# A delta-rule loop over 64 tokens: the state read two steps back, outer products on GpSimd, the read-out on VectorE and GpSimd

## What is computed

```
u_t = v_t - f_t (S_{t-1} k_t)
S_t = f_t S_{t-1} + b_t u_t k_t^T
o_t = S_t q_t
```

## Time and profile before

| what | us |
|---|---|
| runs, lowest / median / highest | 1332.24 / 1338.23 / 1342.46 |
| profiled execution: span from its first to its last instruction | 1330.3 |
| busy in the span: TensorE / VectorE / ScalarE / GpSimd | 1176.4 / 797.4 / 585.9 / 510.6 |
| the loop's groups: line 1787 / 1790 / 1792 on VectorE, 128 of each | 87.4 / 93.1 / 87.8 |
| line 1457 / line 1466 on TensorE | 138.3 / 134.3 |
| line 1858 / line 1862 on GpSimd | 149.2 / 78.0 |
| fades, line 1692 on ScalarE | 104.0 |

### The profile page before, as it was taken

How to read it: one execution, slowest core, us unless ns; L and a number is a source line. 1 busy time by engine, 2 the same in 40 slices (tenths; PEclk the granted TensorE clock), 3 DMA queues, 4 the chain that set the end, 5 groups by cost and what they waited for, 6 DMA issues and landing times. The chain is left out here.

```text
span 1330.3 us, 25816 instructions
## 1 busy us (share of the span) xinstructions
PE 1176.4 (88%) x9667; PEld 923.4 (69%) x9667; DVE 797.4 (60%) x1835; ACT 585.9 (44%) x1480; POOL 510.6 (38%) x568
## 2 busy tenths in 40 slices
PE   6999997598999999989699999995899999879975
PEld 4666666598999999963355656664677777667653
DVE  4666665421212212177899999996577677533687
ACT  3445442111121121145677777772344434325455
POOL 0111111132333333254688888884212122101556
PEclk9999999699999999999799999997999999979985
DMA  4111100689888888379000000002000040017611
GB/s 143 45 48 33 49 13 13 257 334 373 327 328 318 323 328 325 118 199 286 36 0 1 1 0 1 1 1 81 11 13 10 10 191 9 2 34 300 204 49 64
DMA packets 82716, 162.30 MB, mean 122 GB/s; under 512 B 42977, under 2 KB 61537, under 8 KB 76577
## 3 DMA queue, kind: packets, MB, share of 16 engines
q1 hardware_dynamic: 63776, 114.44, 25.1%
q0 software_dynamic: 10224, 44.05, 8.6%
q10 hardware_dynamic: 8592, 2.16, 0.8%
HBM read 134.28 MB, written 26.35 MB: 121 GB/s over the span
## 5 line engine op out<-in xcount | busy, mean ns | idle before, releaser
L936 PE MATMUL banks<-rowsT,w_up 128*128 128x128 f32 x1716 | 199.7, 276 | 0.1
L936 PEld LDWEIGHTS banks<-rowsT,w_up 128*128 128x128 f32 x1716 | 196.5, 193 | 0.4 <-DMA w_up<-in_up_w 0.4
L1466 PEld LDWEIGHTS banks<-ys,ident 128*128 128x128 f32 x992 | 125.2, 191 | 95.6 <-POOL ys L1862 66.0
L1858 POOL TENSOR_TENSOR ys<-xT_d,q_by_time 128x1024 f32<-128x1024 f32 x63 | 149.2, 2368 | 36.6 <-ACT xT_d L1596 36.6
L1466 PE MATMUL banks<-ys,ident 128*128 128x64 f32 x992 | 134.3, 290 | 17.7 <-POOL ys L1862 17.6
L1457 PE MATMUL banks<-made,ident 128*128 128x512 f32 x256 | 138.3, 622 | 12.0 <-DVE made L1792 11.9
L1692 ACT ACTIVATE banks<-banks,rate 128x256 f32<-128x256 f32 x256 | 104.0, 444 | 65.4 <-DVE made L1787 65.4
L1105 DVE TENSOR_TENSOR hT<-banks,silu 64x128 f32<-64x128 f32 x39 | 11.0, 283 | 164.8 <-ACT silu L993 164.8
L950 PE MATMUL banks<-w_down,hT 128*128 128x256 f32 x468 | 107.5, 379 | 0.6 <-DVE res L1115 0.6
L1790 DVE TENSOR_REDUCE banks<-made 128x32 f32<-128x544 f32 x128 | 93.1, 728 | 4.4
L878 POOL DMA_DIRECT2D w_down<-in_down_w x39 | 22.4, 574 | 186.6 <-PE banks L950 178.5
(11 more groups left out here) (325 smaller groups left out, 2383.0 us busy)
## 6 DMA issues: line engine op xcount, KB each, us to landing
w_up<-in_up_w SPq DMA_DIRECT2D x39, 1408.0 KB, 5.9
w_down<-in_down_w POOLq DMA_DIRECT2D x39, 768.0 KB, 5.2
inter<-res_x SPq DMA_DIRECT2D x16, 512.0 KB, 3.5
back<-inter SPq DMA_DIRECT2D x15, 512.0 KB, 4.0
patches<-in_patches SPq DMA_DIRECT2D x16, 384.0 KB, 3.3
f<-in_f SPq DMA_DIRECT2D x6, 1024.0 KB, 11.0
ys<-token_rows SPq DMA_DIRECT2D x16, 256.0 KB, 2.9
xn_rows<-xn_all SPq DMA_DIRECT2D x16, 128.0 KB, 1.7
```

The costliest lines, as they stand in the source:

```text
L936: ins = pe.matmul(out[:, m * P:(m + 1) * P], w[:, c, m * P:(m + 1) * P], x[:, c, :], start=(c == 0), stop=(c == 1))
L1466: ins = pe.matmul(o_sum[t % 2], ident[:, :], products[t % 2][:, :, :, n], start=(n == 0), stop=(n == FOLDED - 1))
L1858: pool.tensor_tensor(qs[:, :, :, :], Sc[(t + 1) % 2][:, :, :, :], bcast(qt[:, t, :, :], 2, HD), ALU.mult).then_inc(sem("qs_made"), 1)
```

## The change

- The loop reads the state two steps back. With S_{t-1} = f_{t-1} S_{t-2} + b_{t-1} u_{t-1} k_{t-1}^T put into the first equation, u_t needs S_{t-2} times a key scaled by both decays, plus a "link" number (from f_t, b_{t-1} and the product of neighbouring keys) times u_{t-1}. `prod` gets an 18th column: 16 products, the link term, the value. `prod`, `u` and `outer` become rings of two; `u` moves from PSUM to SBUF.
- Ahead of the loop, GpSimd multiplies neighbouring keys (`multiply_neighbours`, 1008 elements a group), VectorE sums them and makes the link numbers (`link_keys`), two small operations more in `scale_keys`, whose factor for `kb` now comes first; the link numbers take the place of the write rates in `rate`.
- GpSimd makes the outer product of all four groups in one operation, after the link term; it reads out group 3 (256 elements, from a copy that ScalarE makes) two steps behind.
- VectorE reads out groups 0 to 2 from PSUM in one operation (768 elements), three steps behind; the fold is gone.
- TensorE sums sixteen products for two tokens at once (128 columns), eight matmuls a step; ScalarE stores two tokens at once.
- ScalarE's fade comes after the product that reads the same state; it turns the queries of all four groups. The last two tokens are read out whole by VectorE. The chunks of squares move from 17, 34, 51 to 18, 36, 52.

The diff, cut to what the text speaks of:

```diff
-CUTS = (0, 17, 34, 51)
+CUTS = (0, 18, 36, 52)
 IN_STEPS = len(CUTS) - 1
-LASTS = ((CUTS[-1], TOK - 2), (TOK - 2, TOK))
+TAIL = 2
+LASTS = ((CUTS[-1], TOK - TAIL), (TOK - TAIL, TOK))
 LAST = TOK - CUTS[-1]
-FOLDED = HD // 2
+ROW = HD + 2
+DIRECT = CG - 1
...
+    link = rate[:, :, 0, :]
-    o_sum = [banks[:, b, 0:CG * HD].rearrange("p (g v) -> p g v", g=CG) for b in (5, 7)]
-    u = banks[:, 4, 0:CG * HD].rearrange("p (g v) -> p g v", g=CG)
+    o_sum = [banks[:, b, 0:2 * CG * HD] for b in (5, 7)]
...
         def add_outer(t, h):
...
+            if t:
+                pe.wait_ge(sem(f"faded{h}"), t)
+            pe.wait_ge(sem("outer_made"), t + 1)
+            pe.matmul(S[t % 2][:, halves[h], :, :], ident[:, :], outer[t % 2][:, halves[h], :, :], start=False,
                       stop=True, skip_group_check=True).then_inc(sem(f"state{h}"), 1)
...
+        def sum_pair(n, half):
+            if half == 0:
+                pe.wait_ge(sem("q_made"), 2 * n + 2)
+                pe.wait_ge(sem("q_copy_made"), 2 * n + 2)
+                if n > 1:
+                    pe.wait_ge(sem("o_made"), n - 1)
+            for k in range(HD // 2 * half, HD // 2 * (half + 1)):
+                ins = pe.matmul(o_sum[n % 2].rearrange("p (s n) -> p s n", s=2), ident[:, :],
+                                products[:, n % 2, :, :, k], start=(k == 0), stop=(k == HD - 1))
+            if half:
+                ins.then_inc(sem("o_summed_pair"), 1)
...
             for h in range(2):
                 add_outer(t, h)
-                if t >= 2:
-                    sum_folded(t - 2, h)
+            if t >= 3:
+                sum_pair((t - 3) // 2, (t - 3) % 2)
...
+        def place_values(t):
+            act.copy(prod[t % 2][:, :, :, HD + 1], v[:, :, :, t]).then_inc(sem("values_placed"), 1)
+        def fade(t, h):
+            act.wait_ge(sem(f"state{h}"), t + 1)
+            act.wait_ge(sem(f"prod_made{h}"), min(t + 2, TOK))
+            if t >= 2:
+                act.wait_ge(sem("q_made"), t - 1)
+            for g in (2 * h, 2 * h + 1):
+                ins = act.activation(S[t % 2][:, g, :, :].rearrange("p v k -> p (v k)"),
+                                     S[(t + 1) % 2][:, g, :, :].rearrange("p v k -> p (v k)"), ACT.Copy,
+                                     scale=rate[:, g, 1, t:t + 1])
+            ins.then_inc(sem(f"faded{h}"), 1)
+        def copy_last_group(j):
+            act.wait_ge(sem("state1"), j + 2)
+            if j >= 2:
+                act.wait_ge(sem("q_copy_made"), j - 1)
+            act.copy(Sc[j % 2], S[j % 2][:, DIRECT, :, :]).then_inc(sem("state_copied"), 1)
+        def store_pair(n):
+            act.wait_ge(sem("o_summed_pair"), n + 1)
+            act.copy(o[:, :, :, 2 * n:2 * n + 2], o_sum[n % 2].rearrange("p (s g d) -> p g d s", s=2, g=CG)
+                     ).then_inc(sem("o_made"), 1)
...
+        place_values(0)
+        place_values(1)
+        turn_queries(3)
         for t in range(TOK):
...
+            if t + 2 < TOK:
+                act.wait_ge(sem("u_made"), t + 1)
+                place_values(t + 2)
+            if t:
+                fade(t, 0)
+                fade(t, 1)
+            if 0 < t < TOK - 1:
+                copy_last_group(t - 1)
+            if t >= 5 and t % 2:
+                store_pair((t - 5) // 2)
...
         def scale_keys(g):
             dve.wait_ge(sem(f"rates{g}"), 16)
+            if g >= 2:
+                dve.wait_ge(sem("kb_made"), g - 1)
+            by_rate, by_rn = f[:, 0, g % 2, :], f[:, 1, g % 2, :]
+            dve.scalar_tensor_tensor(out=by_rn, in0=rate[:, g, 0, :], scalar=1.0, in1=rn[:, g, :],
+                                     op0=ALU.add, op1=ALU.mult).then_inc(sem("kb_scale"), 1)
             once.mark(dve.tensor_scalar(rate[:, g, 1, :], rate[:, g, 1, :], 0.5, 0.5, ALU.mult, ALU.add))
             once.settle()
-            once.mark(dve.scalar_tensor_tensor(out=f[:, 0, g % 2, :], in0=rn[:, g, :], scalar=-1.0, in1=rate[:, g, 1, :],
+            once.mark(dve.scalar_tensor_tensor(out=by_rate, in0=rn[:, g, :], scalar=-1.0, in1=rate[:, g, 1, :],
                                                op0=ALU.mult, op1=ALU.mult))
+            dve.wait_ge(sem("kb_scale"), g + 1)
             once.settle()
...
+            once.mark(dve.tensor_tensor(link[:, g, 1:], by_rate[:, 1:], by_rn[:, 0:TOK - 1], ALU.mult))
+            once.settle()
+            once.mark(dve.tensor_tensor(by_rate[:, 1:], by_rate[:, 1:], rate[:, g, 1, 0:TOK - 1], ALU.mult))
+            once.settle()
             once.mark(dve.tensor_tensor(ka[:, :, g, :].rearrange("p t d -> p d t"), k[:, g, :, :],
-                                        bcast(f[:, 0, g % 2, :], 1, HD), ALU.mult))
+                                        bcast(by_rate, 1, HD), ALU.mult))
+        def link_keys(g):
+            dve.wait_ge(sem("neighbours"), g + 1)
+            dve.tensor_reduce(n2[:, g, 1:], dots.rearrange("p d t -> p t d"), AX.X, ALU.add
+                              ).then_inc(sem("dots_summed"), 1)
+            dve.wait_ge(sem("dots_summed"), g + 1)
+            once.mark(dve.tensor_tensor(link[:, g, 1:], link[:, g, 1:], n2[:, g, 1:], ALU.mult))
...
+            link_keys(g)
+        once.mark(dve.memset(prod[0][:, :, :, HD], 0.0))
+        once.settle()
+        def read_keys(t):
+            if t >= 2:
+                dve.wait_ge(sem("u_made"), t - 1)
+            for h in range(2):
+                dve.wait_ge(sem(f"state{h}"), max(t, 1))
+                dve.tensor_tensor(prod[t % 2][:, halves[h], :, 0:HD], S[t % 2][:, halves[h], :, :],
+                                  bcast(ka[:, t, halves[h], :], 2, HD), ALU.mult).then_inc(sem(f"prod_made{h}"), 1)
+        def read_queries(j):
+            n = j // 2
+            dve.wait_ge(sem("state_copied"), j + 1)
+            if n >= 2:
+                dve.wait_ge(sem("o_summed_pair"), n - 1)
+            dve.tensor_tensor(products[:, n % 2, j % 2, 0:DIRECT * HD, :].rearrange("p (g v) k -> p g v k", g=DIRECT),
+                              S[j % 2][:, 0:DIRECT, :, :], bcast(qt[:, j, 0:DIRECT, :], 2, HD), ALU.mult
+                              ).then_inc(sem("q_made"), 1)
+        def read_last(j):
+            for h in range(2):
+                dve.wait_ge(sem(f"state{h}"), j + 2)
+                dve.wait_ge(sem(f"faded{h}"), TOK - 1)
+            once.mark(dve.tensor_tensor(prod[j % 2][:, :, :, 0:HD], S[j % 2], bcast(qt[:, j, :, :], 2, HD), ALU.mult))
+            once.settle()
+            dve.tensor_reduce(o[:, :, :, j], prod[j % 2][:, :, :, 0:HD], AX.X, ALU.add).then_inc(sem("last_o"), 1)
         for t in range(TOK):
+            if t == 3:
+                dve.wait_ge(sem("q_turned"), CG)
+            if t >= 3:
+                read_queries(t - 3)
+            read_keys(t)
             for h in range(2):
...
                 dve.wait_ge(sem(f"prod_made{h}"), t + 1)
...
+            dve.wait_ge(sem("values_placed"), t + 1)
+            if t:
+                dve.wait_ge(sem("corrected"), t)
+            if t >= 2:
+                dve.wait_ge(sem("outer_made"), t - 1)
+            dve.tensor_reduce(u[t % 2], prod[t % 2], AX.X, ALU.add).then_inc(sem("u_made"), 1)
+        read_queries(TOK - 3)
+        dve.wait_ge(sem("u_made"), TOK)
+        read_last(TOK - 2)
+        read_last(TOK - 1)
...
+        def multiply_neighbours(g):
+            pool.wait_ge(sem(f"chain_k{g}"), 16)
+            if g:
+                pool.wait_ge(sem("dots_summed"), g)
+            pool.tensor_tensor(dots, k[:, g, :, 1:], k[:, g, :, 0:TOK - 1], ALU.mult).then_inc(sem("neighbours"), 1)
+        def read_copy(j):
+            n = j // 2
+            pool.wait_ge(sem("state_copied"), j + 1)
+            if n >= 2:
+                pool.wait_ge(sem("o_summed_pair"), n - 1)
+            pool.tensor_tensor(products[:, n % 2, j % 2, DIRECT * HD:CG * HD, :], Sc[j % 2],
+                               bcast(qt[:, j, DIRECT, :], 1, HD), ALU.mult).then_inc(sem("q_copy_made"), 1)
...
+        multiply_neighbours(0)
         scale_keys(0)
+        multiply_neighbours(1)
         load_chain(pool, 1, "q", q)
         scale_keys(1)
         load_chain(pool, 2, "v", v)
+        multiply_neighbours(2)
         scale_keys(2)
         load_chain(pool, 2, "q", q)
+        multiply_neighbours(3)
         scale_keys(3)
...
+        pool.wait_ge(sem("kb_made"), CG)
+        for t in range(TOK):
+            pool.wait_ge(sem("u_made"), t + 1)
+            if t + 1 < TOK:
+                pool.tensor_tensor(prod[(t + 1) % 2][:, :, :, HD], u[t % 2], bcast(link[:, :, t + 1], 2, HD), ALU.mult
+                                   ).then_inc(sem("corrected"), 1)
+            if t >= 2:
+                for h in range(2):
+                    pool.wait_ge(sem(f"state{h}"), t)
+            pool.tensor_tensor(outer[t % 2], bcast(kb[:, t, :, :], 2, HD), bcast(u[t % 2], 3, HD), ALU.mult
+                               ).then_inc(sem("outer_made"), 1)
+            if t == 2:
```

(37 more changed lines are left out.)

82 lines of the change are left out of this document (18 added, 64 removed).

## The result

The changed kernel takes 1432.13 us (median of four runs, 1427.18 to 1436.77) against 1340.35 of the kernel before beside it: ratio 1.071, 95% interval 1.066 to 1.075. It is slower by 92 us; the forecast was 1334. The profiled execution's span is 1425.2, 94.9 longer than the 1330.3 before, and four views show where that lies.

A forecast was written before the change was run, and what follows sets the result against it. VectorE was taken to bound the kernel before. Loop -23.9, ahead of it +19.6 and behind it 0 made -4.3 on the 1330.3 span, 1326.0; with 7.9 up to the median, 1334 us; own range 1322 to 1346, with rivals 1314 to 1364.

The forecast's parts named there:

- Sixteen records in 1.78: TensorE's read-out in the loop: sixteen records of 128 columns, one every 0.111 us, 1.78 us a step.
- The rival on the slow side: TensorE pays for columns 64 bytes apart in `sum_pair`: records over 0.111 us, 1438 at 0.216; chance 0.15.
- The rest of TensorE and the loop: Steps of 3.60 us, 4.15 with squares; first to last sum 244.3 against 268.2, so -23.9 us.
- Ahead of the loop: GpSimd holds VectorE's small operations, so the loop starts 16.2 us late and TensorE's first sum comes +19.6.
- No hold: Rival ahead of the loop: VectorE's small operations run beside GpSimd's, loop starts 6 us late; 1324; chance 0.14.
- Dearer outer product: Rival in the loop: GpSimd's outer product paces from 2.7 us; at 3.89 the time is 1405; chance 0.07.
- Behind the loop: From the last read-out sum to the scaling of outputs: same operations as before, 4.85 us, so a change of 0.
- Two steps back frees nothing: Rival in the loop: the sum still waits a whole round; a step of 4.17 us, 1358; chance 0.01.
- Engines that don't mesh: Rival in the loop: waits between near-equal engines add 0.3 us a step, 1353; chance 0.07.

The follow-up runs named there:

- adjacent columns: Changed kernel with TensorE's sixteen records reading 128 neighbouring columns of the same buffer, so other products are added up; 1325.92 us.
- the cure: Changed kernel with products laid out k outermost, VectorE and GpSimd turning on the reading side; 1327.42 us, ratio 0.992; with `kb` released last as well 1315.87, ratio 0.985.

## Why the prediction was wrong, point by point

- **Sixteen records in 1.78: the step that failed.** The forecast took 0.111 a record "because 64 columns 64 bytes apart come as often as 68 side by side do". The measured spacing is 3.48 / 16 = 0.217, the upper bound of 0.216. The comparison could not carry the conclusion: both rows sat on what a record takes at least (1.87 for sixteen of 32 columns, 1.93 of 64), under which any price up to 0.109 a record is out of sight. The text saw that a small one could hide there and still took the low end of its bounds. The price was not small, it was as large as the cover: 64 x 1.7 ns.
- **The rival on the slow side** was this mechanism, with 1438 at its upper bound; 1432 came. It was given 0.15. Doubling the old spacing with the width, the plainest reading of a row whose floor isn't known, would have led to it.
- **The rest of TensorE and the loop was right.** With neighbours to read, a step is 3.50 (forecast 3.60, paced by TensorE and not by VectorE), and first to last sum takes 240.1 (244.3). With squares it is 4.17 where six records of them stand in it and 3.95 where four do (adjacent columns, line 1467 at 760.36, 764.53 and 768.48); the forecast's 4.15 for all came from 0.59 for four, which holds the run-out of the last.
- **Ahead of the loop: +19.25 for +19.6,** and for the reason given: in each of the four groups a small operation of 2.4 us beside `kb`. Undoing it brought 7.5 us from the first reduction to the loop. *No hold* is refuted. That the sum came within 0.4 us is luck in part. The first reduction began 1.8 us later than the forecast had it (605.12 for 603.35; 603.87 to 607.91 in the six traces with this order), and the way from there to the first sum was 2.1 shorter (55.6 for 57.75): the product of neighbours took 1.87 instead of 2.33 and held nothing in the last three groups, and the outer product was cheaper, as below.
- **GpSimd:** outer product 1.93 (forecast 2.38), link 0.31 (0.37), read-out 0.73 (0.61); together 2.97, where the forecast's three prices add up to 3.36 (its 3.35 was to hold a wait as well); none of it on the bound. *Dearer outer product* is refuted.
- **VectorE:** sum 1.35 (1.37), read-out 0.95 (0.95). **Behind the loop:** 4.82 (4.85).
- *Two steps back frees nothing* is refuted by the steps of 3.50 in the runs with the cure; a loop of one step with all else equal was not tried. *Engines that don't mesh*: no sign of it.

The mechanism of the change was thus right, and with the cure its gain is 0.8%; one term, forecast at half its size, stood on the engine that the change made the bound.

## What to carry to other kernels

A row shows an operand's price only if that price isn't hidden under a floor of its instruction: before a width or a count is doubled, ask what the narrow row was bound by, and bound the wide one by scaling the whole spacing. When a tile is laid out, let the engine on the bound read neighbours, and put the turn where it is free; here that was VectorE's read of PSUM. And release work on GpSimd behind VectorE's small operations, not in front of them.

## What was not expected of the hardware

- TensorE's read price steps from nothing at 8 bytes between columns (1.98 for sixteen records of 128) to its full size at 16 (3.79), and doesn't grow beyond (3.88 at 32 bytes, 3.65 at 64). Steps between 8 and 16 bytes were not tried.
- VectorE reads PSUM 64 bytes apart at no cost (957 against 953 ns for 768 elements), but writes to SBUF 512 bytes apart at 1531.
- GpSimd's product of 1024 takes 1.93 when one source repeats in the innermost place, and 2.35 to 2.36 with a repeat further out or none.
